# Two narrow self attentions: query and key stacks of 49 fp32r rows, two heads in the two row halves of the array, stacks built in DRAM

## The chip, the cores and the metric

The kernel runs on one core of one Trainium2 chip. The metric is the device time of one execution in microseconds (us); lower is better. The core has five engines with instruction queues of their own: PE (TensorE, matrix multiplication), ACT (ScalarE, activations), DVE (VectorE), POOL (GpSimd) and SP (SyncE, which issues all transfers here). A queue runs strictly in order, and semaphores order the queues among each other.

## The reference, cut to what matters

Four transformer layers follow one another on x of shape (2, 1024, 256). Each is a self attention, a cross attention to 77 context rows, and a two-layer perceptron, each on a modulated layer norm. Layers 0 and 1 are narrow (16 heads of 16 channels), layers 2 and 3 wide (16 heads of 64). This is the self attention of layer 1; that of layer 0 is the same computation:

```python
def _attn(q, k, v):
    q = q.reshape(q.shape[0], q.shape[1], H, HD).transpose(0, 2, 1, 3)   # H = 16, HD = 16
    k = k.reshape(k.shape[0], k.shape[1], H, HD).transpose(0, 2, 1, 3)
    v = v.reshape(v.shape[0], v.shape[1], H, HD).transpose(0, 2, 1, 3)
    scores = jnp.einsum('bhnd,bhmd->bhnm', q, k) * HD ** (-0.5)
    p = jax.nn.softmax(scores, axis=-1)
    o = jnp.einsum('bhnm,bhmd->bhnd', p, v)
    return o.transpose(0, 2, 1, 3).reshape(o.shape[0], o.shape[2], D)
h = _ln(x, ln1_w, ln1_b) * (1 + sc1[:, None, :]) + sh1[:, None, :]
qkv = h @ Wqkv + bqkv
q, k, v = jnp.split(qkv, 3, axis=-1)
x = x + _attn(q, k, v) @ Wos + bos
```

## The kernel before

The whole network is one program. A planner writes one list of steps, `order`: every step has a time in units of a stage's progress, `plan.put(time, ...)`, the list is sorted by these times, and each engine's program walks through the same list and emits what is its part of each step. So the order of each queue is fixed when the kernel is built, and is not changed by how long anything takes.

A narrow self attention is 16 units: two batch rows, four groups g of four heads, two halves of 512 queries. For one unit:

- `max` (32 a unit): a 128 x 512 tile of scores for the running maximum, made on PE (L1091) into one of three PSUM banks, the ring `attn` = banks 4, 5, 7; DVE reduces it to a column (L1761) and frees the bank. `mjoin` joins the two halves of the keys, `mturn` transposes the 16 columns to rows, and SP copies the negated maxima into a row of the query stack.
- `score` (16 a unit): per block of 128 keys (kt) and pair of heads (pr), two 128 x 512 matmuls (the helper `acc`, L1015) into a pair of the banks 0 to 3, followed by the exponential on ACT (L1469, 1,024 columns). The maximum is subtracted by the extra row: row 96 of the query stack holds it, row 96 of the key stack holds ones.
- `av` (8 a unit): the weighing by V (L1194), one 128 x 32 tile in f32 for each of four heads, side by side in the four column quarters of the array.
- `fin`, `sums16`, `norm`, `proj` (L1479, L1213, L1221, L1246 on PE and ACT, L1838 and L1854 on DVE): normalisation and output projection, one unit later, in the same ring of three banks.

The maxima of unit n are spread over the time of unit n - 1 (`max(n - 1.3, 0)` to `n - 0.3`), so on PE they stand between the scores and weighings of the unit before. In the same stretch stand the projections of queries and keys of the second batch row (`p16`), those of the values (`val16`, L1719 on DVE) and the layer norms of the next stage.

Precision: queries and keys are f32 values cut in three bf16 parts; six products of parts are kept. `p16` makes the parts: ACT the first (L1416), DVE the rest and the second (L1711, L1714), POOL the third (L1990). `keep16` writes them to the DRAM tensor `scr_n` (L2115), six transfers of 256 KB for each batch row and chunk of 128 channels. `stack16` reads them back as a stack for four heads: six blocks of 16 rows (`G6Q`, `G6K` say which part stands in which block), 96 rows in all, twelve transfers of 128 KB (L2127). Two stack buffers are used in turn; group g waits for the last score of group g - 2. A row of ones in the key stack is set by DVE (`begin16`, `fill16`: L1681, L1684).

The cross attentions of these layers use the same tiles, with bf16 stacks of 97 rows, and their plan is appended to that of the self attention. The wide layers use fp32r, in which a matmul of 512 columns takes f32 data in one pass; their maxima are L1087. The perceptrons' matmuls are L1015 (up) and L1324 (down), also in fp32r.

## Time and profile before

| | before |
|---|---|
| median of 3 runs | 4522.99 us (4517.64 to 4530.47) |
| profiled execution, its own time | 4537.6 us |
| its span, first to last instruction | 4535.8 us |
| mean granted clock of PE | 0.948 |
| busy: PE, DVE, ACT, POOL | 4070.6, 3010.2, 2076.4, 1349.6 us |

The profile is of one execution of its own. Durations are taken from it, and its own time stands 0.3% above the median of the runs, so a difference worked out in it has to be put on the median. Busy shares are averages over stages that differ much. Matmuls are pipelined: the record of one is longer than its distance to the next, so paces are read from the starts of groups, not from mean durations. PEclk is the granted clock as a share of 2.4 GHz.

### The profile page before, as it was taken

How to read it: one execution, taken by the hardware profiler on the slowest of the kernel's cores; microseconds unless marked ns; L12 is line 12 of the kernel's file. 1: busy time of each engine (PE TensorE's matmuls, PEld its weight loads, DVE VectorE, ACT ScalarE, POOL GpSimd, SP SyncE). 2: the span in 40 equal slices, each digit the busy share in tenths (PEclk: the TensorE clock that was granted, in tenths of full speed). 3: DMA queues.
4: the chain of work that ended last, by engine and by line, in shares of the span. 5: the costliest groups of instructions: out<-in, count | busy, mean ns of one | idle time of the engine just before them, and what ended most of it. 6: DMA issues, size and time to landing. Idle time of an engine off the chain costs nothing.

```text
span 4535.8 us, 55477 instructions
## 1 busy us (share of the span) xinstructions
PE 4070.6 (90%) x20428; PEld 2486.0 (55%) x20428; DVE 3010.2 (66%) x4405; ACT 2076.4 (46%) x3756; POOL 1349.6 (30%) x664
## 2 busy tenths in 40 slices
PE   7999979799998888998999967888999999997889
PEld 5343357634335675555555545666555555546668
DVE  5888755688885666777777844345677777764355
ACT  2656645255564543443444435553444344435541
POOL 1100011100001035655555543321444444441120
PEclk8999989899998999999999978998999999998999
DMA  4223230312323142331333222323232222214220
GB/s 131 39 43 49 44 70 24 56 30 43 47 44 63 32 88 63 66 65 39 65 66 66 63 65 67 70 61 63 69 70 60 67 66 66 60 47 108 68 54 20
DMA packets 151983, 269.28 MB, mean 59 GB/s; under 512 B 34090, under 2 KB 67812, under 8 KB 150688
## 3 DMA queue, kind: packets, MB, share of 16 engines
q1 hardware_dynamic: 151712, 265.72, 27.9%
q8 instruction: 163, 2.67, 0.3%
q14 instruction: 108, 0.88, 0.1%
HBM read 105.01 MB, written 29.64 MB: 30 GB/s over the span
## 4 chain that ended last, share of the span: by engine, by line
PE 38%; DVE 8%; ACT 4%; POOL 4%; issue 4%; SPq 3%; DMA 1%; POOLq 0%; DVEq 0%; ACTq 0%
PE PS L1015 19%; PE PS L1194 7%; PE PS L1087 4%; PE PS L1236 4%; PE PS L1324 2%; DVE t L1757 2%; SPq L2173 2%; ACT t L1490 1%; DVE PS L1829 1%; SPq L2190 1%; POOL t L2035 1%; PE PS L1118 1%; POOL t L2022 1%; POOL t L2008 1%; PE PS L1204 1%
## 5 line engine op out<-in xcount | busy, mean ns | idle before, releaser
L1015 PE MATMUL PS<-t 128*128 128x512 f32 (+4 forms) x7896 | 1988.9, 384 | 160.4 <-ACT t L1469 24.8
L1469 ACT ACTIVATE t<-PS 128x512 f32<-128x512 f32 (+2 forms) x1600 | 1166.9, 750 | 1124.7 <-PE PS L1015 1118.3
L1015 PEld LDWEIGHTS PS<-t 128*128 128x128 f32 (+2 forms) x7896 | 1253.8, 188 | 708.9 <-issue 253.5
L1194 PE MATMUL PS<-t 128*32 128x512 f32 (+2 forms) x4352 | 809.7, 610 | 0.2
L1757 DVE TENSOR_REDUCE t<-PS 128x1 fp32r<-128x1024 f32 x512 | 622.0, 1220 | 281.4 <-PE PS L1087 275.8
L1761 DVE TENSOR_REDUCE t<-PS 128x1 f32<-128x512 f32 x1024 | 651.4, 684 | 73.1 <-PE PS L1091 70.7
L2035 POOL TENSOR_TENSOR t<-t 128x1024 f32<-128x1024 f32 x256 | 617.6, 2412 | 133.6 <-ACT t L1469 106.9
L1091 PE MATMUL PS<-t 96*128 96x512 bf16 x1024 | 370.3, 394 | 34.8 <-DVE t L1761 14.3
L1087 PE MATMUL PS<-t 128*128 128x512 f32 x1024 | 339.9, 415 | 58.8 <-DVE t L1757 36.4
L2031 POOL TENSOR_TENSOR t<-t 128x1024 f32<-128x1024 f32 x64 | 155.0, 2422 | 734.4 <-PE PS L1204 442.1
L1194 PEld LDWEIGHTS PS<-t 128*32 128x32 f32 (+2 forms) x4352 | 170.7, 122 | 329.1 <-issue 324.4
L1972 POOL TENSOR_TENSOR t<-t 128x2048 f32<-128x2048 f32 x24 | 112.0, 4668 | 788.1 <-DMA t<-in_rows 528.6
L1091 PEld LDWEIGHTS PS<-t 96*128 96x128 bf16 x1024 | 97.1, 98 | 358.2 <-DVE t L1761 135.4
L1236 PE MATMUL PS<-t 128*128 128x256 f32 x1024 | 260.3, 399 | 27.5 <-DVE t L1742 10.9
L1850 DVE TENSOR_TENSOR t<-PS,t 128x1024 f32<-128x1024 f32 x128 | 156.3, 1221 | 166.3 <-PE PS L1236 166.3
L1087 PEld LDWEIGHTS PS<-t 128*128 128x128 f32 x1024 | 195.5, 197 | 127.6 <-DVE t L1757 53.3
L1236 PEld LDWEIGHTS PS<-t 128*128 128x128 f32 x1024 | 197.7, 199 | 69.2 <-issue 23.9
L1829 DVE RECIPROCAL PS<-PS 128x256 f32<-128x256 f32 x128 | 224.7, 1755 | 11.8 <-PE PS L1204 11.8
L1324 PE MATMUL PS<-t 128*128 128x256 f32 x1536 | 219.0, 295 | 10.4 <-DVE t L1946 5.8
L1324 PEld LDWEIGHTS PS<-t 128*128 128x128 f32 x1536 | 207.6, 199 | 22.8 <-DVE t L1946 5.5
L1490 ACT ACTIVATE t<-PS,t 128x77 f32<-128x77 f32 x512 | 159.3, 325 | 132.3 <-DVE t L1797 132.1
L1946 DVE TENSOR_TENSOR t<-t 128x512 fp32r<-128x512 f32 x128 | 113.6, 888 | 138.8 <-ACT t L1572 137.5
(131 smaller groups left out, 3804.9 us busy)
## 6 DMA issues: line engine op xcount, KB each, us to landing
t<-t SPq DMA_DIRECT2D x640, 128.0 KB, 2.5
t<-scr_n SPq DMA_DIRECT2D x288, 128.0 KB, 6.4
t<-t SPq DMA_DIRECT2D x128, 256.0 KB, 3.8
scr_n<-t SPq DMA_DIRECT2D x72, 256.0 KB, 2.3
t<-t SPq DMA_DIRECT2D x256, 64.0 KB, 2.0
t<-in_L_Wg SPq DMA_DIRECT2D x16, 768.0 KB, 4.6
t<-in_L_W SPq DMA_DIRECT2D x36, 256.0 KB, 3.2
t<-in_L_Wo SPq DMA_DIRECT2D x64, 128.0 KB, 2.5
```

The costliest lines, as they stand in the source:

```text
L1015: ins = e.matmul(out, l, r, start=i == 0, stop=i == len(terms) - 1, tile_position=tp)
L1087: ins = e.matmul(o[:, 512 * h:512 * h + 512], u.smq[j][qt], u.smk[j][h], start=True, stop=True)
L1091: e.matmul(o, u.smq[j][qt], u.smk[j][half], start=True, stop=True).then_inc(*bank_full[k].inc(nth))
L1194: ins = e.matmul(banks[S.ot][wd * j:wd * j + wd, :], u.v[j][kt], P[0:S.pr, j, :], start=kt == 0, stop=kt == S.nkt - 1, tile_position=(0, w ...
L1236: ins = e.matmul(o[:, 256 * q:256 * q + 256], S.OR[n % 2][:, 128 * q:128 * q + 128], u.wo[:, :], start=True, stop=True)
L1324: ins = e.matmul(banks[4 + q][:, 0:D], l, r, start=m == 0 and t == 0, stop=m == 7 and t == 2)
L1469: e.activation(dst, src, ACT.Exp, scale=S.L.scale).then_inc(*expd.inc((S.i, i)))
L1490: ins = e.activation(S.PQ[n % 3][:, j, t, :], o[:, 256 * t + CT * b:256 * t + CT * b + CT], ACT.Exp, bias=S.NM[n % 3][:, at], accum_out=S. ...
L1757: e.tensor_reduce(S.MT[m % 2][:, S.nqt * j + qt:S.nqt * j + qt + 1], o, AX.X, ALU.max, negate=True).then_inc(*bank_free[k].nth(nth))
L1761: e.tensor_reduce(S.NMX[:, 4 * j + qt, half:half + 1], o, AX.X, ALU.max).then_inc(*bank_free[k].nth(nth))
L1829: e.reciprocal(o[:, hs], o[:, hs]).then_inc(*recip_made.inc((S.i, n, h)))
L2035: e.tensor_tensor(S.AP_[:, :, :], S.AP_[:, :, :], P[1][:, :, :], ALU.add).then_inc(*pool_summed.inc((S.i, n, kt)))
```

## The change

Only the self attentions of layers 0 and 1 change:

- Queries and keys are cut in two fp32r parts in place of three bf16 ones. Three products of parts are kept, so a stack has 48 rows and one for the maximum: 49. Two heads of a group stand in one stack buffer, one in rows 0 to 48, one in rows 64 to 112. A matmul on the second takes tile rows 64 to 127 of the array, one on the first rows 0 to 63. This holds for scores and maxima both.
- The maxima are ordered so that the two heads of a pair alternate. `mjoin` has two buffers for its input, and the maxima are turned to rows in f32.
- `p16` needs ACT for the first part and one DVE instruction for the second; the cast on DVE and the instruction on POOL are gone. The parts go to one of three block buffers `NB`, and a block is written to DRAM after each half of 512 columns, not after both.
- `keep16` writes each part straight to its places in a DRAM tensor `scr_s` that is laid out as the stacks are, (batch row, q or k, head, 64, 1024): six transfers of 256 KB in f32 for each half, twelve for each chunk. `stack16` is two transfers of 1 MB.
- Row 48 of `scr_s` (zeros for queries, ones for keys) is filled at the program's start, rows 49 to 63 by copies of it within DRAM at the beginning of layer 0. The row of ones that DVE set is gone.

```diff
+    STKD = dram("scr_s", (NB, 2, 16, 64, N))
...
-            S.NMX = sbt(c, [128, 16, 2])
+            S.NMX = [sbt(c, [128, 16, 2]) for _ in range(2)]
...
+            S.QK = [q[:, :, :, :].rearrange("p a (x y) n -> p a x (y n)", x=2).bitcast(F32R) for q in S.QKB]
+            S.NB = [flat[:, 2048 * i:2048 * i + 2048].rearrange("p (s n) -> p s n", s=4) for i in range(3)]
...
+                    own = [slice(64 * (j % 2), 64 * (j % 2) + 49) for j in range(4)]
+                    u.smq = [[buf[own[j], 0, j // 2, q0 + 128 * t:q0 + 128 * t + 128] for t in range(4)] for j in range(4)]
+                    u.mrow = [f(buf[64 * (j % 2) + 48:64 * (j % 2) + 49, 0, j // 2, q0:q0 + 512]) for j in range(4)]
...
-                    u.smk = [[buf[0:96, 1, j, 512 * h:512 * h + 512] for h in range(2)] for j in range(4)]
-                    u.st = [[[(buf[0:97, 1, j, 128 * kt:128 * kt + 128], buf[0:97, 0, j, q0:q0 + 512])]
+                    u.smk = [[buf[own[j], 1, j // 2, 512 * h:512 * h + 512] for h in range(2)] for j in range(4)]
+                    u.st = [[[(buf[own[j], 1, j // 2, 128 * kt:128 * kt + 128], buf[own[j], 0, j // 2, q0:q0 + 512])]
...
-            out = [("max", S, m, j, qt, half) for j in range(S.nh) for qt in range(4) for half in range(2)]
+            out = [("max", S, m, 2 * pr + jj, qt, half) for pr in range(2) for qt in range(4) for half in range(2)
+                   for jj in range(2)]
...
+        return [x for half in range(2) for x in (("p16", S, b, ch, half, 0), ("p16", S, b, ch, half, 1), ("keep16", S, b, ch, half))]
...
+                    i = 4 * b + 2 * ch + half
+                    if i >= 3:
+                        w.wait_ge(nat_out[i % 3], (S.i, i - 3))
+                    dst = S.NB[i % 3][:, 2 * qk, :]
...
-                e.memset(S.QK[1][96:97, 1, :, :], 1.0).then_inc(*zeroed.inc(S.i))
...
+                    e.scalar_tensor_tensor(block[:, 2 * qk + 1, :], o, nat16_bias(S, qk, ch), f(block[:, 2 * qk, :]),
+                                           ALU.add, ALU.subtract).then_inc(*bank_free[k].nth(nth))
...
+                            e.dma_start(STKD[b, qk, :, 49:64, :], STKD[b, qk, :, 48:49, :].broadcast_to([16, 15, N])
+                                        ).then_inc(*rest_filled[b].inc(b, 16))
...
+                    for slot, part in enumerate(((0, 0, 1), (0, 1, 0))[qk]):
+                        e.dma_start(STKD[b, qk, 8 * ch:8 * ch + 8, 16 * slot:16 * slot + 16, 512 * half:512 * half + 512],
+                                    f(S.NB[i % 3][:, 2 * qk + part, :])).then_inc(*nat_out[i % 3].inc((S.i, i), 16))
...
+                    src = STKD[g // 4, qk, 4 * (g % 4):4 * (g % 4) + 4, :, :].rearrange("(x y) r n -> (y r) x n", y=2)
+                    e.dma_start(f(S.QK[g % S.nbuf][:, qk, :, :]), src).then_inc(*stacked[g % S.nbuf].inc((S.i, g), 16))
```

The first place is on PE, inside layer 0's self attention, a stretch of one weighing to another. Before (L1091 a maximum, L1015 x2 a pair of scores, L1194 the weighing, L1213 the sums):

```order
L1194 MATMUL PS<-t 32x512 x4
L1091 MATMUL PS<-t 128x512
L1015 MATMUL PS<-t 128x512 x2
L1091 MATMUL PS<-t 128x512
L1213 MATMUL PS<-t 128x4 x4
L1015 MATMUL PS<-t 128x512 x2
L1091 MATMUL PS<-t 128x512 x2
L1194 MATMUL PS<-t 32x512 x4
```

The same place in the change, where L1105 is a maximum, L1029 x2 a pair of scores, L1208 the weighing and L1227 the sums:

```order
L1208 MATMUL PS<-t 32x512 x4
L1105 MATMUL PS<-t 128x512
L1029 MATMUL PS<-t 128x512 x2
L1105 MATMUL PS<-t 128x512
L1227 MATMUL PS<-t 128x4 x4
L1029 MATMUL PS<-t 128x512 x2
L1105 MATMUL PS<-t 128x512 x2
L1208 MATMUL PS<-t 32x512 x4
```

The steps stand where they stood. New is the part of the array: a pair of scores takes the lower, then the upper half, and the maxima alternate between the halves in their own order, whatever stands between them; the sums and the weighing take all rows.

The second place is on SP, at the beginning of layer 0's self attention: the first rows of queue traffic up to the first stack. Before (L2115 writes the parts, L2127 reads the stack):

```order
L2095 DMA t<-in_L_Wo 128x1024 [waits rest3,rest2,rest4,rest1,rest0]
L2097 DMA t<-in_vrows 128x256
L2115 DMA scr_n<-t 128x1024 [waits nat_0] x2
L2115 DMA scr_n<-t 128x1024 [waits nat_1] x2
L2115 DMA scr_n<-t 128x1024 [waits nat_2] x2
L2127 DMA t<-scr_n 16x4x1024 [waits nat_kept0]
L2127 DMA t<-scr_n 16x4x1024 x11
```

In the change (L2138 fills rows 49 to 63, L2162 writes the parts, L2180 reads the stack):

```order
L2130 DMA t<-in_L_Wo 128x1024 [waits rest3,rest2,rest4,rest1,rest0]
L2132 DMA t<-in_vrows 128x256
L2138 DMA scr_s<-scr_s 16x15x1024 [waits row_filled]
L2138 DMA scr_s<-scr_s 16x15x1024
...
L2162 DMA scr_s<-t 8x16x512 [waits bank_free5,nat_0]
L2162 DMA scr_s<-t 8x16x512 x2
L2162 DMA scr_s<-t 8x16x512 [waits bank_free7,nat_0]
...
L2180 DMA t<-scr_s 128x2x1024 [waits rest_filled0,nat_out1,nat_out0]
L2180 DMA t<-scr_s 128x2x1024
```

Four fills (two of them left out here) now stand ahead of the first write, the writes of two half blocks are twelve in place of six, and the stack is two transfers that wait for both half blocks and for the fill.

## Rows read from the trace of the kernel before

**Rows 1.** The page: busy time; then the chain that ended last, by line.
```profile
PE 4070.6 (90%) x20428; PEld 2486.0 (55%) x20428; DVE 3010.2 (66%) x4405; ACT 2076.4 (46%) x3756; POOL 1349.6 (30%) x664
...
PE PS L1015 19%; PE PS L1194 7%; PE PS L1087 4%; PE PS L1236 4%; PE PS L1324 2%; DVE t L1757 2%; SPq L2173 2%; ACT t L1490 1%; DVE PS L1829 1%; SPq L2190 1%; POOL t L2035 1%; PE PS L1118 1%; POOL t L2022 1%; POOL t L2008 1%; PE PS L1204 1%
```

**Rows 2.** Windows: stretch, length, busy us of each engine, clock, DMA share, GB/s.
```profile
110.26:131.50 21.24, 17.56 (x81) 4.46 (x79) 20.97 (x45) 9.80 (x10) 4.51 (x1) 1.00 0.61 74
110.26:581.73 471.47, 454.65 (x2612) 183.68 (x2611) 389.43 (x698) 288.26 (x324) 29.66 (x18) 1.00 0.28 43
905.00:1385.00 480.00, 461.21 (x2606) 184.54 (x2605) 392.30 (x701) 288.77 (x321) 25.16 (x17) 0.98 0.25 39
...
600.00:700.00 100.00, 82.05 (x557) 57.88 (x557) 59.72 (x133) 41.11 (x55) 18.41 (x12) 0.85 0.35 69
```

**Rows 3.** Groups by form, 200 to 500 us: count, busy us, mean ns, idle before.
```profile
L1761 DVE TENSOR_REDUCE t<-PS 128x1 f32<-128x512 f32 x323 | 206.4, 684 | 20.1 <-PE PS L1091 19.4
L1091 PE MATMUL PS<-t 96*128 96x512 bf16 x323 | 113.8, 383 | 4.9 <-DVE t L1711 2.3 <-DVE t L1761 2.2
L1015 PE MATMUL PS<-t 97*128 97x512 bf16 x322 | 94.5, 379 | 0.0
L1015 PEld LDWEIGHTS PS<-t 97*128 97x128 bf16 x323 | 31.4, 101 | 25.7
L1015 PEld LDWEIGHTS PS<-t 128*128 128x128 f32 x92 | 14.4, 189 | 6.1 <-DVE t L1761 3.4 <-ACT t L1519 0.7
```

**Rows 4.** Timeline of PE, layer 0's self attention: start us, us, instruction.
```profile
299.64 0.39 PE L1091 MATMUL PS<-t 96*128 96x512 bf16 x1
299.96 1.06 PE L1194 MATMUL PS<-t 128*32 128x512 f32 x8
300.95 0.98 PE L1015 MATMUL PS<-t 128*128 128x256 f32 x6
...
310.07 0.60 PE L1015 MATMUL PS<-t 97*128 97x512 bf16 x2
310.51 0.38 PE L1091 MATMUL PS<-t 96*128 96x512 bf16 x1
```

**Rows 5.** Timeline of PE: fp32r in layer 3's perceptron and attention; sums of layer 0.
```profile
4425.00 2.97 PE L1015 MATMUL PS<-t 128*128 128x512 f32 x12
4427.81 0.60 PE L1036 MATMUL PS<-t 128*128 128x128 f32 x4
...
3702.56 1.94 PE L1194 MATMUL PS<-t 128*64 128x512 f32 x8
3704.43 0.74 PE L1015 MATMUL PS<-t 128*128 128x512 f32 x2
3705.01 0.63 PE L1087 MATMUL PS<-t 128*128 128x512 f32 x2
...
302.65 0.95 PE L1213 MATMUL PS<-t 128*128 128x4 f32 x8
```

**Rows 6.** Timeline of SP, DVE and PE at the start of layer 0.
```profile
52.41 4.50 SPq L2115 DMA_DIRECT2D scr_n<-t  x6
58.75 5.48 SPq L2127 DMA_DIRECT2D t<-scr_n  x12
...
70.31 3.47 DVE L1684 MEMSET t<- 1x4096 bf16 x1 [0.91 <-issue]
...
75.75 0.65 PE L1091 MATMUL PS<-t 96*128 96x512 bf16 x1
```

**Rows 7.** Windows of 5 us at the program's start, columns as in rows 2.
```profile
15.00:20.00 5.00, 3.50 (x17) 3.51 (x17) 1.97 (x7) 1.46 (x7) 2.57 (x1) 1.00 1.04 425
...
55.00:60.00 5.00, 4.40 (x24) 3.65 (x22) 4.90 (x8) 2.58 (x6) 3.55 (x5) 1.00 0.68 250
...
65.00:70.00 5.00, 2.21 (x11) 1.95 (x10) 4.03 (x16) 0.00 (x0) 1.80 (x2) 0.80 1.09 117
```

**Rows 8.** Timeline of SP and PE at the start of layer 1's self attention.
```profile
847.44 5.48 SPq L2127 DMA_DIRECT2D t<-scr_n  x12
...
862.54 1.89 PE L1091 MATMUL PS<-t 96*128 96x512 bf16 x4 [8.04 <-DMA t<-scr_n]
```

145 lines of the change are left out of this document (88 added, 57 removed).

## The prediction

> **What bounds the kernel now.** I read the page first: TensorE is busy for 90% of the span and leads the chain that ended last, while VectorE is at 66% [rows 1]. Those are averages over twelve stages, and the edit touches two of them, the self attentions of layers 0 and 1. So next I cut the span from the first to the last score of each [rows 2]: 471.5 us and 480.0 us, together 951.5 us for 32 units, 29.7 us a unit. There TensorE is busy 96% (454.7 of 471.5), VectorE 82 to 83% (389.4 and 392.3), ScalarE 61%, and the clock is granted in full. The bound is TensorE, with VectorE 65 us of each stage behind it. The groups of a steady stretch say what fills them [rows 3]: TensorE with maxima (L1091) and scores (L1015, 97 rows), VectorE with the reductions of the maxima (L1761).
>
> How high VectorE can go is shown by the first unit of layer 0, where a statistics pass falls on top of dense maxima: 20.97 of 21.24 us busy, 98.7%, and TensorE only 17.56 [rows 2]. There VectorE is the bound already, and nothing that TensorE saves helps.
>
> **The change part by part.** *Scores and maxima.* In each stage 512 scores and 480 of the 512 maxima lie between first and last score: 992 matmuls. In bf16 they follow one another at 0.22 us (a pair from 310.07 to 310.51) [rows 4]; I take 0.217, so they hold TensorE for 215 us. Removed: 215.
>
> What replaces them is one fp32r matmul each, of 49 rows, on rows 0 to 48 or 64 to 112. Two neighbours in different halves can run together, two in the same half cannot. A matmul of 512 fp32r columns takes 0.234 us (twelve in 2.81, from 4425.00 to 4427.81) [rows 5]. No matmul of before uses half of the rows, so whether the halves overlap is not in this trace. The nearest thing is the column quarters of the weighing by V (L1194): eight instructions, two rounds of four heads, in 0.99 us [rows 4], where eight that ran one after the other at even one cycle a column would need 1.7 us. Hence I take full overlap. The maxima are not always beside their partner, since scores and weighings stand between them: a typical run is maximum, two scores, two maxima, two scores, maximum. Walking through the program's order with the halves as the code gives them, starting each matmul with its predecessor if its half is free, gives 585 turns for the 992, not 496. 585 x 0.234 = 137 us. Added: 137.
>
> Three things work against it. First the weight loads: 189 ns for fp32r, 101 ns for bf16 [rows 3]. They pipeline: eight f32 loads with four-column matmuls pass in 0.95 us, about 0.11 us each [rows 5]. Two a pair are 0.22, as long as the pair itself, so I let them hide, with nothing to spare. Second, behind a change of tile shape a load has nothing to hide under: in the wide layer two fp32r scores after a weighing take 0.58 us (3704.43 to 3705.01) against 0.47 at the steady pace, 0.11 more [rows 5]. The program has 218 such runs a stage: 24 us. Third, half-row runs are now a shape of their own beside full-row matmuls (projection, sums, values): 457 changes of shape in place of 280 in layer 0, 436 in place of 296 in layer 1, so some 160 more a stage. A change into the weighing costs 0.10 us (0.32 from 299.64 to 299.96 against 0.22) [rows 4]. Whether one between half and full rows costs that is not shown: between 0 and 0.10, nearest to the weighing's, so 0.10, 16 us.
>
> The Trainium skill (TensorEngine Tiling (Array Packing), Key Properties) says that changing the tiling mode drains the engine, and counts 64 rows as a mode of their own. By that rule the third item stands, and the forecast with it; without it the forecast would be 32 us lower, 4438.
>
> TensorE's load in a stage: 454.7 - 215 + 137 + 24 + 16 = 417 us. Its lower bound, without second and third, is 377; its upper one, without any overlap, is 454.7 - 215 + 992 x 0.234 + 40 = 512.
>
> *VectorE.* The reductions stay, 32 a unit with records of 684 ns that overlap a little [rows 3]. One cast per projected block goes, two memsets of a single row a stage go (3.47 us each [rows 6]), neither to speak of inside the core. So its load stays at 389 and 392 us, its floor 389.4/0.987 = 395 and 397. Now 417 and 389 stand close, and both meet at the same three banks: a maximum at the head of TensorE's queue waits for a bank that VectorE frees, and all scores stand behind it. Before, with 65 us between them, TensorE idled for 17 us. With 30 between them I take 22 more than the load, 440 a stage; the bounds are 397 and 471. Gain of the cores: 951.5 - 880 = 71 us; I keep 65, since the first unit and those with the next normalisation are VectorE's already.
>
> *Start of layer 0.* Four copies within DRAM, 1 MB each, now go into the same queue ahead of all else, each half block of both kinds is written as six transfers of 256 KB (3 MB for the first chunk, was 1.5), and a stack is 2 MB in two transfers (was 1.5 MB in twelve). Before, writes began at 52.4, stack reads at 58.75, and the first maximum ran at 75.75 [rows 6], reads going at 117 GB/s with the queue full, 16 partitions at a time; big loads reach 425, block writes at least 250 [rows 7]. The new reads fill 128 partitions with 4 KB runs, so I take 250 and 8 us in place of 15. Fills and writes bring 5.5 MB more, 22 us at 250; about 6 of them fit before 52.4, as the writes wait for ScalarE and VectorE until then. 22 - 6 - 7 = 9, plus 3 as copying inside DRAM is not shown at all: 12 us later. Bounds -5 (425 GB/s) and +35 (117). ScalarE also holds the fourth half block until the first has landed; that lies under the wait for the stack.
>
> *Start of layer 1.* Before, stack reads from 847.4, first maximum at 862.54 with 8.04 us idle for the DMA [rows 8]. The reads get shorter by 7, the writes double but start a half block earlier: -3 us.
>
> *Maxima rows.* Behind a 1.5 MB half block in the queue the row of maxima lands late once or twice: +3.
>
> Sum: -65 + 12 - 3 + 3 = -53. The profiled execution took 4537.6 us, the median of three runs 4523.0, 0.3% less: 4484.6 becomes 4470.
>
> **The rivals.** *VectorE's floor is reached.* Speaks for it: 98.7% in the first unit, where TensorE's waits cost VectorE nothing. It needs a TensorE load near 377, that is free changes of shape. Cores at 395 and 397 give -159, in all 4380. Chance 0.12.
>
> *The halves do not overlap* (or loads and streaming share a path, with both loads 0.11 in front of 0.234). This one ends slower: load 512, 57 us a stage more, 4537.6 + 114 + 12 = 4664, in median terms 4650. It decides from the turn: break-even is (215 - 40)/585 = 0.30 us. Speaks for it: two loads are already as long as a turn, and no half-row matmul is on record. Against it: the column quarters. Chance 0.17, with turns between 0.31 and 0.47.
>
> *The block writes run at half the rate.* Their target is cut in 8 heads of 16 rows where it was 128 rows in one; if fewer of the 16 DMA engines take part, 3 MB at 125 in place of 250 GB/s cost 12 us more before the first maximum of layer 0, and some 3 us at each of the later mixed stretches: 4537.6 - 65 + 12 + 12 + 6 = 4503 (the 3 us of layer 1's start and of the rows cancel), in median terms 4488. Nothing in the rows tells the two apart. Chance 0.25. The Trainium skill (DMA: Bandwidth & Descriptors, "Why a DMA increments its semaphore by 16 and not by 1") says that a transfer uses the largest number of engines up to 16 that divides the slowest dimension of both sides; no run here shows it yet.
>
> *The clock, or bank ping-pong, eats the gain.* Where TensorE waits more, as from 600 to 700 us (82% busy), the granted clock is 0.85 on average [rows 2], a mix of 1.2 and 2.4 GHz. A TensorE that waits for VectorE at every bank might lose 5%, 21 us a stage; with the starts that leaves 4510 to 4530. Against it: in the first unit it waits for VectorE all the time and the clock is 1.00. Chance 0.09.
>
> **How the numbers follow.** Forecast with its own range of 4410 to 4508: 0.37, and with half-rate writes, in the same range, 0.25; floor 0.12; gain eaten 0.09; slower 0.17. This kernel's measurement can tell 0.3% (14 us) from no change. Faster 0.74, same 0.09, slower 0.17. The range goes from 4390, just above the floor case, to 4560, which is a turn of about 0.34 us; outside lie the rest of the floor case and most of the slow one, two in ten.
>
> **What would show it.** In the profile after: half-row matmuls of a pair starting together and about 0.24 us a turn; cores of about 440 us with TensorE near 95% and VectorE near 89%; the first maximum of layer 0 near 88 us; waits of the weight loads on VectorE's reductions longer than before. Wrong would be: scores one after the other, VectorE's share unchanged, or a core of over 470 us. The likeliest error is the cost of the closeness of two engines around three banks, 22 us a stage, which I chose and did not read.

## The result

| | before | after |
|---|---|---|
| median | 4526.73 us (4 runs, 4517.64 to 4535.87) | 4585.84 us (4 runs, 4570.11 to 4591.3) |
| ratio, 95% interval | | 1.0127 (1.0111 to 1.0142) |
| profiled execution | 4537.6 us, span 4535.8 | 4590.6 us, span 4588.4 |
| mean granted clock | 0.948 | 0.936 |

Slower by 59 us (the interval of the ratio lies clear of 1), where 53 us less was forecast. The page of the changed kernel:

```profile
PE 4096.7 (89%) x20428; PEld 2541.8 (55%) x20428; DVE 2983.1 (65%) x4370; ACT 2075.1 (45%) x3756; POOL 1313.1 (29%) x632
L1105 PEld LDWEIGHTS PS<-t 49*128 49x128 f32 x1024 | 176.4, 201 | 385.0 <-DVE t L1790 202.8
```

The same loads before, at that time L1091:

```profile
L1091 PEld LDWEIGHTS PS<-t 96*128 96x128 bf16 x1024 | 97.1, 98 | 358.2 <-DVE t L1761 135.4
```

TensorE's share hardly moves. The wait that matters is that of the weight loads of the maxima: they stand 202.8 us behind VectorE's reductions (L1790), where before it was 135.4. The cores, cut from first to last score as in [rows 2], and two stretches inside them (the columns are those of [rows 2]):

```profile
121.01:617.94 496.93, 467.09 (x2619) 208.89 (x2621) 390.00 (x690) 288.24 (x325) 20.46 (x10) 0.95 0.18 55
929.84:1444.21 514.37, 483.05 (x2611) 217.29 (x2613) 392.18 (x692) 288.46 (x322) 15.89 (x9) 0.91 0.16 49
125.00:155.00 30.00, 28.31 (x97) 10.76 (x100) 22.27 (x49) 12.46 (x13) 2.01 (x1) 0.51 0.06 25
300.00:400.00 100.00, 97.44 (x584) 45.74 (x584) 82.64 (x140) 58.29 (x64) 0.00 (x0) 1.00 0.17 61
```

Layer 0's core takes 496.9 us (was 471.5), layer 1's 514.4 (was 479.7, cut at its own first and last score; the window of [rows 2] is rounded to 480). Of the 52.6 us between the two profiled spans, 10.8 lie ahead of the first score of layer 0, 25.5 in its core, -12.0 between the cores, 34.7 in layer 1's core and -6.3 behind it. Two things stand out. VectorE's work is what it was, 390 and 392 us, but its share fell. And the clock: 0.51 from 125 to 155 us, where [rows 2] had 1.00 from 110 to 131 (and the kernel before had 1.00 from 125 to 155 us too), and 0.91 over layer 1's core. From 300 to 400 us it was granted in full. The stretch of [rows 3], from 200 to 500 us, at a clock of 0.98:

```profile
L1105 PE MATMUL PS<-t 49*128 49x512 f32 x302 | 119.6, 467 | 14.8 <-DVE t L1790 6.5 <-DVE t L1728 4.9
```

There 302 maxima were made where before 323 were, and the mean record of one grew from 383 to 467 ns. The counts make the loss look larger than it is at full clock, since the stretch holds 13.6 us at half the clock and an idle time of 4.24 us, shown below.

Cut into units, the two cores show where the time went. A unit runs here from the exponential (ScalarE's instruction behind a pair of scores) that opens it to the one that opens the next, so the sums differ by 1 to 2 us from the cores above. Units are counted from 0:

| us | before | changed | more |
|---|---|---|---|
| layer 0: 12 units with the full clock in both | 352.1 | 358.9 | 6.8 |
| layer 0: unit 2 | 31.4 | 38.2 | 6.9 |
| layer 0: units 0, 10 and 12, clock 0.61, 0.89, 0.94 in the changed kernel, 1.00 before | 90.4 | 101.7 | 11.3 |
| layer 1: 10 units with the full clock in both | 291.1 | 296.3 | 5.2 |
| layer 1: unit 2 | 31.9 | 44.1 | 12.1 |
| layer 1: units 0, 9 to 12, clock 0.59 to 0.94, before 0.90 to 1.00 | 157.7 | 174.6 | 16.9 |

At full clock the changed kernel is slower by 0.5 us a unit; most of the loss lies in a few units. Unit 2 is a case of its own. There VectorE's cast L1689, 0.42 us in the median, took 3.87 us beside an instruction on GpSimd, and ended 0.3 us after it; TensorE stood behind the reduction that followed:

```profile
195.52 4.54 POOL L2001 TENSOR_TENSOR t<-t 128x2048 f32<-128x2048 f32 x1 [68.51 <-DMA t<-in_rows]
196.47 3.87 DVE L1689 CAST t<-t 128x512 fp32r<-128x512 f32 x1
201.72 0.49 PE L1105 MATMUL PS<-t 49*128 49x512 f32 x1 [4.24 <-DVE t L1790]
```

In layer 1 it was L1691, 4.90 us where 0.69 is usual, with 4.99 us of idle TensorE, and both times the clock stood at 0.50 afterwards. In unit 2 of the kernel before no VectorE instruction was held like this, and with the interleaved stacks (below), whose matmuls are the same, none either: the unit took 32.2 and 32.1 us there. So some 18 us of the two cores hang on whether two instructions of other engines meet, and not on the array. No run was made to test it.

The start, first SP's queue and the first maximum, then the DMA (answers to [rows 6, 7]):

```profile
45.77 3.37 SPq L2138 DMA_DIRECT2D scr_s<-scr_s  x4
49.75 16.33 SPq L2162 DMA_DIRECT2D scr_s<-t  x12
75.73 0.90 SPq L2180 DMA_DIRECT2D t<-scr_s  x2
...
83.79 0.79 PE L1105 MATMUL PS<-t 49*128 49x512 f32 x1 [2.78 <-DMA t<-scr_s]
```

```profile
65.00:70.00 5.00, 0.45 (x3) 0.46 (x3) 1.26 (x2) 1.42 (x3) 0.00 (x0) 0.50 0.53 204
70.00:75.00 5.00, 5.00 (x25) 5.00 (x25) 0.15 (x1) 1.45 (x6) 0.00 (x0) 0.50 0.48 186
```

The first maximum runs at 83.8 us (was 75.75). The twelve writes hold the queue until 66, and while the rest of them runs the DMA share is 0.53 and 0.48, as with about half of the 16 engines at work, at 204 and 186 GB/s.

How a run of half-row matmuls goes, in a stretch at full clock. Behind a weighing (L1208) the run begins at 355.08, the next weighing at 357.38; between them nine half-row matmuls, maxima (L1105) and scores (L1029); PEld are the weight loads:

```profile
354.33 3.77 DVE L1790 TENSOR_REDUCE t<-PS 128x1 f32<-128x512 f32 x6
355.08 0.19 PEld L1105 LDWEIGHTS PS<-t 49*128 49x128 f32 x2 [0.84 <-DVE t L1790]
355.08 0.51 PE L1105 MATMUL PS<-t 49*128 49x512 f32 x2
355.19 0.19 PEld L1029 LDWEIGHTS PS<-t 49*128 49x128 f32 x2
355.42 0.40 PE L1029 MATMUL PS<-t 49*128 49x512 f32 x2
355.66 0.18 PEld L1105 LDWEIGHTS PS<-t 49*128 49x128 f32 x1 [0.28 <-DVE t L1790]
355.66 0.49 PE L1105 MATMUL PS<-t 49*128 49x512 f32 x1
355.66 0.29 PEld L1029 LDWEIGHTS PS<-t 49*128 49x128 f32 x2
355.66 0.72 PE L1029 MATMUL PS<-t 49*128 49x512 f32 x2
356.36 0.18 PEld L1105 LDWEIGHTS PS<-t 49*128 49x128 f32 x1 [0.40 <-DVE t L1790]
356.36 1.09 PE L1105 MATMUL PS<-t 49*128 49x512 f32 x2
356.95 0.18 PEld L1105 LDWEIGHTS PS<-t 49*128 49x128 f32 x1 [0.41 <-DVE t L1790]
357.38 0.64 PE L1208 MATMUL PS<-t 128*32 128x512 f32 x4
```

The halves do overlap: the two scores of 355.42 are followed at 355.66, 0.24 us a pair, as forecast. But the run takes 2.30 us and not 5 turns x 0.234 = 1.17 plus a load. At 356.36 one maximum goes, and its partner is held until VectorE (L1790) frees a bank: its load starts at 356.95, 0.19 us pass before it may stream, and only then 0.234 us of matmul. The pair cost 1.02 us. VectorE, in the first row, took six tiles in 3.77 us, 0.63 us each.

### The profile page after: what moved, and what is told of

The parts are those of the page before. It is cut to its first block, busy times and chain, and to the rows that moved or that the text cites. A ratio compares the mean times of both kernels' runs of the same rounds, so it can differ in the third digit from the quotient of the medians.

```text
span 4588.4 us, 55383 instructions
## 1 busy us (share of the span) xinstructions
PE 4096.7 (89%) x20428; PEld 2541.8 (55%) x20428; DVE 2983.1 (65%) x4370; ACT 2075.1 (45%) x3756; POOL 1313.1 (29%) x632
## 4 chain that ended last, share of the span: by engine, by line
PE 61%; DVE 16%; ACT 7%; issue 5%; SPq 4%; POOL 4%; DMA 3%; DVEq 0%; POOLq 0%; ACTq 0%
PE PS L1029 25%; PE PS L1208 13%; PE PS L1105 5%; DVE t L1790 4%; PE PS L1101 4%; PE PS L1250 4%; PE PS L1338 3%; PE PS L1260 2%; DVE t L1784 2%; SPq L2226 2%; PE PS L1235 1%; SPq L2243 1%; PE PS L1227 1%; ACT t L1497 1%; ACT t L1518 1%
## 5 line engine op out<-in xcount | busy, mean ns | idle before, releaser
L1029 PE MATMUL PS<-t 128*128 128x512 f32 (+4 forms) x7896 | 1985.8, 394 | 165.5 <-ACT t L1497 26.4
L1029 PEld LDWEIGHTS PS<-t 128*128 128x128 f32 (+2 forms) x7896 | 1292.1, 200 | 668.1 <-issue 278.2
L1208 PE MATMUL PS<-t 128*32 128x512 f32 (+2 forms) x4352 | 828.7, 628 | 0.4 <-ACT t L1497 0.4
L1790 DVE TENSOR_REDUCE t<-PS 128x1 f32<-128x512 f32 x1024 | 648.8, 683 | 115.9 <-PE PS L1105 110.8
L1105 PE MATMUL PS<-t 49*128 49x512 f32 x1024 | 419.5, 501 | 53.3 <-DVE t L1790 19.2
L1105 PEld LDWEIGHTS PS<-t 49*128 49x128 f32 x1024 | 176.4, 201 | 385.0 <-DVE t L1790 202.8
L1208 PEld LDWEIGHTS PS<-t 128*32 128x32 f32 (+2 forms) x4352 | 171.7, 123 | 316.4 <-issue 311.3
```

The costliest lines, as they stand in the source:

```text
L1029: ins = e.matmul(out, l, r, start=i == 0, stop=i == len(terms) - 1, tile_position=tp)
L1105: e.matmul(o, u.smq[j][qt], u.smk[j][half], start=True, stop=True).then_inc(*bank_full[k].inc(nth))
L1208: ins = e.matmul(banks[S.ot][wd * j:wd * j + wd, :], u.v[j][kt], P[0:S.pr, j, :], start=kt == 0, stop=kt == S.nkt - 1, tile_position=(0, w ...
L1790: e.tensor_reduce(S.NMX[m % 2][:, 4 * j + qt, half:half + 1], o, AX.X, ALU.max).then_inc(*bank_free[k].nth(nth))
```

## The experiments

Times stand beside 4585.8 us for the changed kernel and 4520 to 4527 us for the kernel before, timed again with each; ratios are to the latter. Cores are spans from first to last score, as above. "At full clock" compares, in one profile each, only units to which both kernels had the full clock granted.

### What overlap and the clock are worth

**Both heads of a pair in one half.** Heads 1 and 2 of each group change places; the column quarters of the weighing follow.

```diff
-                    own = [slice(64 * (j % 2), 64 * (j % 2) + 49) for j in range(4)]
+                    own = [slice(64 * (j // 2), 64 * (j // 2) + 49) for j in range(4)]
```

> Heads 0 and 1 of a group share one row half, heads 2 and 3 the other, so both matmuls of a pair use the same rows; the alternation of the maxima is lost too. 815 turns a stage in place of 585, the same 218 and 212 runs and the same changes of shape. Theory 'the halves do overlap and the overlap is worth what I forecast': 230 turns x 0.234 = 54 us more a stage, about 4586 + 108 = 4694. Theory 'the overlap is there, but TensorE's turns are not what bounds the core (banks, weight loads behind a change of shape, the clock)': less than 50 us in all, 4600 to 4635. Theory 'they never overlapped': no change within 0.3%.

**Full rows.**

```diff
-                    own = [slice(64 * (j % 2), 64 * (j % 2) + 49) for j in range(4)]
+                    own = [slice(0, 128) for j in range(4)]
```

> Each score and each maximum reads all 128 rows of its buffer, so both heads' products are summed: the scores are not the reference's, only the time is read. No half-row shape is left (992 turns, each alone; changes of shape back near 280 and 296). Theory 'half-row matmuls let the granted clock fall': from 100 to 200 us the clock comes back from 0.75 to 0.95 or more, and the stretch from 900 to 1000 us too; the first unit of layer 0 takes no longer than before. Theory 'the clock falls for another reason (fp32r, DMA)': it stays below 0.85 there. Theory 'what eats the gain is the entry into a half-row run, 0.43 us in place of 0.22': with the entries gone, 407 more turns (95 us a stage) are paid for by 218 entries x 0.2 (44) and the clock (20), net +30 a stage, about 4640. Theory 'banks and VectorE bound the core': within 20 us of 4586.

Measured: 4809.5 us (ratio 1.062) with one half, 4569.4 (1.011) with full rows. First the one half, cores and the stretch from 125 to 155 us, then the same of full rows:

```profile
120.52:728.77 608.25, 596.65 (x2620) 287.51 (x2622) 393.20 (x690) 290.74 (x325) 20.42 (x10) 0.76 0.15 45
1050.97:1669.75 618.78, 601.58 (x2612) 288.22 (x2614) 398.36 (x692) 290.51 (x321) 15.85 (x9) 0.75 0.13 40
125.00:155.00 30.00, 29.41 (x94) 12.82 (x92) 21.67 (x48) 12.28 (x13) 1.85 (x1) 0.50 0.06 22
```

```profile
119.68:617.00 497.32, 482.90 (x2617) 273.47 (x2616) 394.08 (x691) 288.66 (x324) 20.54 (x10) 0.99 0.18 55
929.91:1424.00 494.09, 481.66 (x2604) 272.17 (x2603) 390.66 (x692) 288.50 (x321) 16.40 (x9) 0.99 0.16 51
125.00:155.00 30.00, 27.75 (x129) 13.09 (x129) 27.30 (x58) 17.27 (x19) 1.96 (x1) 1.00 0.05 20
```

The two kernels run their matmuls in the same order, up to the quarters of the weighing, and a pair of scores overlaps in neither; with one half a maximum and a score still can, 815 turns against 992. Yet the cores are 608 and 619 us against 497 and 494, and the clock is 0.76 and 0.75 against 0.99. From 125 to 155 us TensorE is busy 98% of the time in the first, so it hardly idles, and is still granted half the clock; with full rows it idles more and has all of it. So here work in one row half goes with the low clock, and not the order of the work. The first expectation named 54 us a stage, 3.4 a unit, for the lost overlap; at full clock it is 1.1 us a unit against the changed kernel (six units of layer 0), some 35 us over 32 units by that estimate, and the rest of the 224 us goes with the low clock. For full rows the price of the entries (4640) missed. What came true is the clock, and the theory that banks and VectorE bound the core: within 20 us of 4586, here 16 us *faster* than the changed kernel. In the cores as a whole overlap brings nothing: 0 in layer 0 (497.3 against 496.9), -20 in layer 1, where the clock is 0.99 against 0.91. At full clock it is worth 0.7 us a unit (358.9 against 366.8 us in twelve units of layer 0), and the clock takes that back.

**Only one of the two in halves.** The maxima on 128 rows, the scores in halves, and the reverse:

```diff
-                    u.smq = [[buf[own[j], 0, j // 2, q0 + 128 * t:q0 + 128 * t + 128] for t in range(4)] for j in range(4)]
+                    u.smq = [[buf[:, 0, j // 2, q0 + 128 * t:q0 + 128 * t + 128] for t in range(4)] for j in range(4)]
```

> Scores stay in row halves, always as pairs; the maxima read all 128 rows (two heads' products summed, only the time is read). No single half-row matmul is left, but more changes between half and full rows. Theory 'half-row matmuls hold the clock down': the 992 are half and half now, so the clock of 125 to 155 us rises above 0.50, to 0.75 or 1.0. Theory 'the entry with a single maximum (0.43 us against 0.33) costs most': within the steady stretch of 300 to 400 us more exponentials than the 64 of the changed kernel. Theory 'every change of shape costs': fewer than 61. Total 4550 to 4600.

> The other way round: maxima in row halves, scores on all 128 rows (summed, only the time is read). The maxima rarely have a partner, so overlap is nearly gone and the changes of shape are the most of all. All theories: slower than the changed kernel; by 20 to 50 us if changes cost 0.1 to 0.2 us each (some 250 more changes a stage against none of the 256 score pairs overlapping, 60 us a stage more), about 4640 to 4700. Theory 'clock': half-row matmuls in every run keep it at 0.50 in the first unit.

Measured: 4635.5 us (1.024) and 4752.7 (1.050), both above their ranges, and at full clock 2.2 and 4.4 us a unit more than the changed kernel (12 and 11 units of layer 0). In the first the clock rises as expected (0.89 from 125 to 155 us, 0.97 over both cores), and the cores still take 529 and 530 us; in the second it is 0.65 from 125 to 155 us, not the 0.50 expected. The timeline of TensorE shows why, at full clock:

```profile
351.90 0.50 PE L1029 MATMUL PS<-t 49*128 49x512 f32 x2
352.33 0.51 PE L1105 MATMUL PS<-t 128*128 128x512 f32 x1
352.77 0.50 PE L1029 MATMUL PS<-t 49*128 49x512 f32 x2
```

The pair takes 0.43 us, the full-row maximum behind it 0.44: 0.234 for the columns and 0.19 for a weight load that nothing covers. Every change of shape between half and full rows exposes the load, in both directions. That agrees with the Trainium skill (TensorEngine Tiling (Array Packing), Key Properties), by which a change of the tiling mode drains TensorE; the size of it, a whole fp32r load, is from these rows.

### Who waits for whom

**VectorE's reductions cut** in both kernels, by reading a quarter of each tile of maxima (the result is not the reference's, only the time is read):

```diff
-                e.tensor_reduce(S.NMX[m % 2][:, 4 * j + qt, half:half + 1], o, AX.X, ALU.max)
+                e.tensor_reduce(S.NMX[m % 2][:, 4 * j + qt, half:half + 1], o[:, 0:128], AX.X, ALU.max)
```

> The changed kernel, with one thing left out: VectorE reads 128 of the 512 columns of each tile of maxima, so that each reduction is about 0.35 us shorter (the maximum is taken over a quarter of the keys; only the time is read). Theory 'VectorE and the three banks eat the gain': with some 170 us a stage less on VectorE the waits for banks go, halves pair up, and the cores come down by 50 us or more each, to about 420 to 450. Theory 'TensorE's own entries into runs and the clock eat it': cores fall by less than 20 us each, and the clock of 125 to 150 us stays 0.50.

> The kernel before with the same shortened reductions: the control. TensorE's load there is 455 of 471 us, so by every theory its cores fall by at most 17 to 20 us each, to about 455, total about 4490. The difference to the changed kernel with the same cut is then TensorE's alone: if that one is faster by 20 us or more, the half rows do gain when VectorE does not stand behind them; if it is slower, they lose on TensorE itself.

Measured: 4460.4 us (0.986) and 4463.5 (0.986). The cores of the changed kernel with the cut, then those of before with it:

```profile
115.78:561.62 445.84, 426.79 (x2619) 203.68 (x2621) 212.58 (x690) 285.63 (x325) 20.49 (x10) 0.98 0.20 61
869.21:1318.91 449.70, 433.26 (x2611) 205.43 (x2613) 208.85 (x692) 286.24 (x322) 15.97 (x9) 0.97 0.19 55
```

```profile
107.08:561.00 453.92, 445.92 (x2617) 185.03 (x2619) 213.21 (x698) 287.50 (x325) 29.73 (x18) 1.00 0.29 45
872.51:1327.79 455.28, 444.93 (x2609) 183.87 (x2611) 214.76 (x700) 287.56 (x322) 25.18 (x17) 1.00 0.27 42
```

This pair settles most. With VectorE's part cut, the changed kernel's core is 446 and 450 us, that of before 454 and 455: what TensorE gains is 8 and 6 us a stage, not 38. VectorE's part is the difference to the uncut kernels: 51 and 65 us with half rows, 18 and 24 us with bf16. The control fell by 63 us where 37 were expected, 42 of them in the cores. The low clock is part of the 51 and 65. It can be set apart by the units of layer 0 that had the full clock in all four profiles (1, 3 to 9, 11, 13 to 15):

| us | these 12 units | the other 4 |
|---|---|---|
| before | 352.1 | 121.8 |
| changed | 358.9 | 139.9 |
| before, reductions cut | 343.9 | 112.0 |
| changed, reductions cut | 332.4 | 115.3 |

At full clock TensorE gains 11.5 us in twelve units, and VectorE's part is 26.5 us with half rows, 8.2 with bf16. So the waits for banks take the gain and 7 us more without any help of the clock.

In the changed kernel with the cut the run between two weighings comes close to what it should have been (TensorE only):

```profile
386.44 0.49 PE L1105 MATMUL PS<-t 49*128 49x512 f32 x1
386.45 0.71 PE L1029 MATMUL PS<-t 49*128 49x512 f32 x2
386.79 0.61 PE L1105 MATMUL PS<-t 49*128 49x512 f32 x2
387.02 0.61 PE L1029 MATMUL PS<-t 49*128 49x512 f32 x2
387.32 0.49 PE L1105 MATMUL PS<-t 49*128 49x512 f32 x1
387.74 1.06 PE L1208 MATMUL PS<-t 128*32 128x512 f32 x8
```

Eight matmuls from 386.44 to 387.74, 1.30 us, where four turns and one load would be 1.13: even here the last maximum comes late, its load at 387.32 behind a reduction. Whether a fourth bank in the ring would close that was not tried. Read from the starts in the same way, runs of eight between two weighings take 1.70 us in the changed kernel (median of nine from 300 to 450 us), with the waits, and 1.84 before (ten).

**Full rows, and one half, with the cut:**

> All 128 rows and the shortened reductions together (two heads summed, the maximum over a quarter of the keys; only the time is read). 992 turns, none overlapping, clock free to be full. If overlap saves what its turns say (407 turns x 0.234 = 95 us a stage, less 0.1 to 0.2 us of extra change at some 160 places), the cores are 446 + 95 - 24 = 517 against 446 with half rows, total about 4590. If the full rows with whole reductions (497) were bound by TensorE already, cutting the reductions moves little: 480 to 497 a stage, total 4540 to 4570, and the overlap is worth only 35 to 50 us a stage.

> Both heads of a pair in one row half, with the shortened reductions. Theory 'half-row matmuls hold the clock down by themselves': the clock of the cores stays near 0.75 and 4780 or more, though TensorE no longer waits for VectorE. Theory 'the clock falls because TensorE waits': it comes to 0.95 or more and the total to about 4600, close to full rows with the same cut.

Measured: 4527.5 us (1.0005) and 4708.9 (1.040). The core of layer 0 with full rows, then with one half:

```profile
110.93:595.19 484.26, 474.62 (x2616) 273.65 (x2617) 217.13 (x690) 288.24 (x324) 20.80 (x10) 1.00 0.19 57
```

```profile
117.49:680.92 563.43, 553.13 (x2620) 271.65 (x2622) 217.51 (x690) 289.17 (x325) 20.48 (x10) 0.82 0.16 49
993.07:1566.92 573.85, 563.24 (x2612) 277.66 (x2614) 215.60 (x692) 289.43 (x322) 15.96 (x9) 0.80 0.14 43
```

So with VectorE's part cut overlap is worth 484 - 446 = 38 us in layer 0, 67 us in the two stages together (4527.5 - 4460.4). And the clock of the one half stays low (0.82, 0.80) with VectorE out of the way, so it is not a matter of waits alone; but in the first unit it was 1.00 here, and 0.50 with whole reductions. Both play a part. Of the expectations for full rows the second held for the core and the worth of overlap, the total is 12 us lower; for one half neither held in full; at full clock it costs 1.9 us a unit there (eight units of layer 0), against the 3.4 of its turns.

**One full-row matmul more per block** in the first two units:

```diff
+                    if not S.cross and n < 2 and pr == 0:
+                        e.matmul(pairs[i % 2][0:S.kr, 0:512], u.full[0], u.full[1], start=True, stop=True)
```

> The changed kernel with one more full-row fp32r matmul of 512 columns ahead of each block's scores in the first two units of both narrow self attentions (32 in all; the scores overwrite its result). It costs 32 x (0.23 + 0.2 to 0.4 for two changes) = 14 to 20 us at full clock. Theory 'half rows alone hold the clock at 0.50 there': from 125 to 155 us it is 0.90 or more, a block takes 4.6 to 5.1 us in place of 5.9, and the total is within 10 us of 4586. Theory 'the clock is low there for other reasons': it stays at 0.50 and the total grows by 20 to 30 us.

Measured: 4611.1 us (1.019), and the clock from 125 to 155 us still 0.51, with TensorE busy for 29.19 of the 30 us.

The theory that I held fell; numbers and clock are those of the other one. Since full rows alone did lift the clock, half rows still have a part in it, but a single full-row matmul for each block doesn't undo it.

### Where the maxima stand

Five placements, to have fewer entries into half-row runs. In the plan the maxima of the next unit were put at the scores' times: in pairs; four behind both pairs of scores of a block; one ahead and three behind; two and two; and at four fixed places. The last four use the interleaved stacks of the next section. The form of the edit, here with one ahead (there the maxima also start with the upper half; the steps that join and turn the maxima move a little in all but the first):

```diff
-                        plan.put(max(n - 1.3, 0), n - 0.3, max_steps(S, n))
+                        slots = list(range(8 * n - 10, 8 * n - 2)) if n > 1 else list(range(6))
+                        for i, k in enumerate(slots):
+                            mine = todo[32 * i // len(slots):32 * (i + 1) // len(slots)]
+                            for x, step in enumerate(mine):
+                                plan.put(k / 8 + (-1e-4 if x < 1 else 1 / 24 + 1e-4), 0, [step])
```

> The maxima stand in the plan in pairs, one of each half, at the time of a pair of scores: 496 turns in place of 585, 155 and 149 runs in place of 218 and 212, 80 fewer changes of shape a stage. Theory 'entries into a run and single turns cost the gain': 89 turns x 0.234 = 21 and 63 entries x 0.2 = 13 us less a stage, together about 4586 - 68 = 4518. Theory 'a pair of maxima waits for two of three banks, one after the other, so VectorE sets the pace': 4570 to 4600, with the waits of the weight loads of the maxima on VectorE's reductions longer. Theory 'the clock': it stays near 0.75 from 100 to 200 us, and only some 30 us are gained.

> The stacks of the interleaved kernel (4570), and the maxima of the next unit stand in the plan four for each block of keys, behind both pairs of scores: one run of S S S S M M M M, then the weighing. 498 turns and 155 runs a stage, as with the pairs of maxima. A wait for a bank then stands behind the scores, not ahead of them, but the fourth maximum always waits for VectorE. Theory 'load of TensorE with exposed loads of 0.19 us, plus waits for banks': load about 448 - 63 x 0.19 - 87 x 0.234 = 416 a stage; if waits stay at 50, cores of 465 and about 4505 in all. Theory 'bursts of maxima starve the ring': cores of 490 or more, 4570 or more.

> The same with one maximum ahead of the scores: M S S S S M M M, the maxima alternating from the upper half so that all eight pair up (4 turns). VectorE reduces the three of the last run under the weighing, and the first one here under the scores. Theory 'entries and bank waits': best of the four, cores of 430 to 460 us, total 4450 to 4500, the clock above 0.95. Theory 'half rows hold the clock down whatever the order': the clock of the cores stays below 0.95 and the total above 4530.

> Two maxima ahead: M M S S S S M M. The second one ahead waits for a bank that VectorE holds, with all scores of the block behind it. Theory 'entries and bank waits': between the two others, 4480 to 4540. If it is the slowest, the wait ahead of the scores is what the pairs of maxima lost on (4644).

> The control: the kernel before (bf16 stacks of 97 rows), with the maxima in the same places as M S S S S M M M. Its matmuls do not overlap, and a run costs only 0.10 us to enter: 63 fewer entries are 6 us a stage. Theory 'the order helps by fewer entries into half-row runs': within 15 us of before, 4510 to 4540. Theory 'the order helps by fewer waits for banks, whatever the rows': faster by 20 us or more too.

> Interleaved stacks; the four maxima of a block stand at fixed places: one behind the weighing, one ahead of the first pair of scores, one between the pairs, one behind the second, so most runs are M M S S M S S M with little clumping. Theory 'entries and clumps of maxima both cost': faster than the 4570 of the interleaved stacks with the old spread, 4520 to 4560. Theory 'any locking of maxima to scores costs more in waits for banks than it saves': 4575 to 4640.

| placement | median, us | ratio |
|---|---|---|
| pairs | 4643.8 | 1.027 |
| none ahead, four behind | 4865.3 | 1.075 |
| one ahead, three behind | 4680.8 | 1.034 |
| two ahead, two behind | 4629.6 | 1.023 |
| fixed places | 4629.9 | 1.023 |
| one ahead, three behind, in the kernel before | 4628.4 | 1.023 |

The theory of entries missed in all of them, by 60 us and more, and always to the slow side; the theory of starved banks named the right range for none ahead and for the fixed places. The interleaved stacks with the even spread take 4570.0, so bunching costs 60 to 295 us. With four in a row TensorE is 85% busy from 300 to 400 us and the clock 0.85:

```profile
300.00:400.00 100.00, 84.83 (x419) 39.11 (x419) 60.88 (x104) 42.41 (x47) 0.00 (x0) 0.85 0.17 40
```

The control shows that this is no matter of half rows: the kernel before loses 104 us by the same bunching. At full clock it is 2 us a unit slower (six units of each core), which over 32 units would be some 60 of the 104, an estimate; the rest lies in units with a lower clock. VectorE needs 0.63 us for each tile and the ring has three banks, so what a planner gives up in even spacing comes back as idle time of TensorE, with the scores queued behind, and in these runs as a lower clock too.

**The old order of the maxima**, eight of one head after one another, in one half:

```diff
-            out = [("max", S, m, 2 * pr + jj, qt, half) for pr in range(2) for qt in range(4) for half in range(2)
-                   for jj in range(2)]
+            out = [("max", S, m, j, qt, half) for j in range(S.nh) for qt in range(4) for half in range(2)]
```

> The changed kernel with the maxima in the order of before, all eight of a head after one another, so in one row half: 719 and 734 turns a stage in place of 585. Theory 'alternation is worth its turns': 134 and 149 turns x 0.234 = 31 and 35 us a stage, about 4652. Theory 'most of the pairs of maxima are broken by the wait for a bank anyway': less than 20 us in all, 4590 to 4606. If the granted clock falls with the work packed less densely in the halves, as with both heads in one half, more: above 4660.

Measured: 4669.8 us (1.033), 84 more than the changed kernel, above the 66 of its turns. But from 125 to 155 us the clock is 0.50, and 0.922 over the whole program against 0.936. At full clock the old order costs 0.35 us a unit (272.4 against 269.2 us in nine units of layer 0, and the same in layer 1), where the lost turns alone would be 2. So at full clock the numbers are those of the second theory, by which most pairs of maxima are broken by the wait anyway, and the bulk of the 84 us goes with the lower clock, as the third had it with its "above 4660".

### The start

**Interleaved stacks.** Row 3r + slot in place of 16 x slot + r makes a write one stride over 128 rows; stacks have 48 rows in DRAM, no fills; the maxima use 48 rows, and a stack is read in four transfers.

```diff
-                        e.dma_start(STKD[b, qk, 8 * ch:8 * ch + 8, 16 * slot:16 * slot + 16, 512 * half:512 * half + 512],
+                        dst = STKD[b, qk].rearrange("h (r s) n -> (h r) s n", s=3)
+                        e.dma_start(dst[128 * ch:128 * ch + 128, slot, 512 * half:512 * half + 512],
```

> Stack rows are interleaved (row 3r + slot) so that a block is written as 128 rows at one stride, not as 8 heads of 16 rows; the DRAM stacks have 48 rows, row 48 of the keys comes from the tile of ones, the maxima use 48 rows, and the 4 MB fill of rows 48 to 63 is gone. Stack reads are 48 rows for each half, 4 transfers of 384 KB. Theory 'the writes run on 8 of 16 engines and the fills stand ahead of them': the DMA share of 0.50 from 65 to 75 us goes to 0.9 or more, the first maximum of layer 0 comes at 68 to 74 in place of 83.8 us, time 4570 to 4577. Theory 'the start is not set by the DMA': first maximum within 2 us of 83.8 and time within 5 us of 4586. The cores stay as they are (497 and 514 us) by all theories.

The same without fills and with short reads, but the writes in 8 heads of 16 rows:

> Stacks of 48 rows in DRAM, no fills, reads of 48 rows in 4 transfers, as in the interleaved kernel, but the writes in their changed form, 8 heads of 16 rows. Theory 'the writes run on 8 engines and set the start': the DMA share is near 0.50 from 60 to 70 us and the first maximum of layer 0 comes at 79 to 83 us, against 73.9 with writes over 128 rows; total 4575 to 4585. Theory 'the fills set it': first maximum within 2 us of 73.9 and total near 4570.

Measured: 4570.0 us (1.011) and 4581.1 (1.012). DMA from 50 to 70 us and the first maximum, interleaved, then in blocks:

```profile
50.00:60.00 10.00, 9.25 (x49) 7.83 (x48) 5.25 (x7) 4.85 (x10) 0.00 (x0) 1.00 0.85 315
60.00:70.00 10.00, 6.92 (x44) 6.50 (x43) 4.62 (x22) 1.54 (x6) 0.00 (x0) 0.77 0.85 132
```

```profile
73.86 0.79 PE L1106 MATMUL PS<-t 48*128 48x512 f32 x1 [6.28 <-DMA t<-scr_s]
```

```profile
50.00:60.00 10.00, 8.16 (x39) 6.74 (x37) 3.75 (x5) 3.12 (x5) 0.00 (x0) 1.00 0.45 142
60.00:70.00 10.00, 6.88 (x32) 6.88 (x33) 1.79 (x4) 3.26 (x10) 0.00 (x0) 0.61 0.45 173
```

```profile
83.23 0.79 PE L1106 MATMUL PS<-t 48*128 48x512 f32 x1 [8.65 <-DMA t<-scr_s]
```

With the block writes the DMA share is 0.45 and the first maximum at 83.2 us; with 128 rows in a write it is 0.85, and the first maximum at 73.9. From 50 to 60 us that is 142 GB/s against 315. The fills and the longer reads matter for 0.6 us there (83.8 with them). A share of about half agrees with the Trainium skill (DMA: Bandwidth & Descriptors, "Why a DMA increments its semaphore by 16 and not by 1"): the number of engines is the largest up to 16 that divides the slowest dimension of both sides, here 8. The trace shows the share, not which engines. Layer 1's core took 499 us in the first of these profiles and 504 in the second, with the matmuls of the changed kernel, which took 514. That core varies with the clock, 0.94 in the first and 0.91 in the changed kernel: units at full clock agree within 0.3 us in the sum of ten, while unit 11 took 29.6 us at 1.00 in the first and 38.5 at 0.69 in the changed kernel, and unit 2 32.1 and 44.1, since the instructions of VectorE and GpSimd do not meet there. So of the 16 us between 4570.0 and 4585.8 the start is 10, and the rest can't be put down to the transfers.

## Why the prediction was wrong, step by step

- **Removed 215, added 137 us (585 turns).** The turn was right: a pair takes 0.24 us, the halves overlap. The rival that denies it is out: at 0.24 us a pair neither loads nor columns wait for the other half. With VectorE's part cut, overlap is worth 38 us in layer 0, not the 95 of its 407 turns.
- **Weight loads and changes of shape, 24 + 16 us a stage.** This step was mis-sized. I took 0.11 us for an entry and 0.10 for one of the 160 further changes, from f32 pairs of full rows and from bf16, where part of the load was already under way. A change between shapes costs the whole fp32r load, 0.19 us (a lone maximum takes 0.43 us, was 0.22 to 0.32 in bf16). With the reductions cut, from the first matmul of each run to the next other one, the 218 runs of layer 0's core take 212.5 us; 582 turns (those on record) x 0.234 = 136 of it are columns, so 76 are left, 0.35 a run. The runs of the kernel before take 235.2 us, 987 x 0.217 = 214 of it columns, 21 left. What lies between the runs grew from 218.7 to 233.4. That is 55 + 15 = 70 us on top of the columns in place of 40, and 453.9 - 214 + 136 + 70 = 446, the measured core. 0.19 a run is 41 of the 76; the others hold late banks, as at 387.32, one stall of 4.2 us like that of unit 2, and two stretches of 6.8 us at half the clock; they were not split further. The low clock of these stretches is in the 446 too. So with VectorE's part cut the core fell by 6 to 8 us, not by 38.
- **Coupling of two engines at three banks, +22 us a stage.** The second step that failed, and the larger one. The 22 were 5 more than the 17 of before; by the cut, VectorE's part grew from 18 to 51 us in layer 0 and from 24 to 65 in layer 1, that is by 34 and 40. I argued from how close the two loads are. What the timeline shows is another mechanism: a bank that is late splits a pair, so that both of its matmuls pay for their columns alone, and the second its load too. That is a cost of half rows at full clock as well: 26.5 us in the twelve units where bf16 had 8.2.
- **The clock, put at nothing in the sum.** The third step. Units 0, 10 and 12 of layer 0 and 0 and 9 to 12 of layer 1 took 11.3 and 16.9 us more, with the clock down to 0.59; that this is the clock's is seen by unit 11 of layer 1, 29.6 us at 1.00 and 38.5 at 0.69 with the same matmuls. Unit 2 of both layers, 6.9 and 12.1 us more, is the meeting of VectorE and GpSimd with the low clock behind it, which no term of the sum had. Without what these units lost, the two cores would still have been 12 us slower and not 71 faster: loads and waits alone had eaten the gain.
- **VectorE's floor** was not approached: 390 of 497 us, 78%.
- **The clock rival (0.09)** named 4510 to 4530 and TensorE's waits as its cause. The clock did fall, but to 0.51 where TensorE was 94% busy, and with half rows in one half where it was 98% busy. So its 0.09 was too low and its price too small. I had argued from the first unit of before, where TensorE waited and the clock was 1.00; that was a stretch of 96 and 97 rows and said nothing of half rows.
- **Start of layer 0, +12 us.** Measured +8 for the first maximum and +10.8 for the first score, but for the wrong reason: I booked 9 for fills and writes and 3 for copying in DRAM, and held half-rate writes for a rival on top. The fills with the longer reads cost 0.6 us, the half rate 9.4. That rival was right in its mechanism, and its price of 12 us near.
- **Start of layer 1, -3 us.** Counted from the end of layer 0's core, the first maximum there comes 9.1 us earlier, and the stretch between the cores is 12.0 us shorter.
- **Maxima rows, +3 us.** Not seen: in neither core does TensorE wait for a transfer.
- **The range.** Its upper end, 4560 us, is by the prediction's own sum a turn of 0.32 us, not 0.34. The measured 4585.8 lies above it with a turn of 0.24, so it was the terms beside the turn that were too narrow.
- **What would show it.** Pairs starting together and the late first maximum came true; cores of 440 us and VectorE at 89% (it was 78) did not, and "a core of over 470 us" was the sign of error that I had named.

No version here that computes the reference's result beats the kernel before. The best of them is the one with interleaved stacks, 4570.0 us.

## What to carry to other kernels

Before splitting the array in halves, count the runs and not the matmuls: each run between other shapes pays one whole weight load, so short runs (here four to five matmuls on average) give much of the overlap back. Then look at what feeds and empties the banks: with VectorE at 390 us beside TensorE's 450, pairs were broken by single late banks. A run with that engine's work cut, of both kernels, tells how much of a gain is TensorE's own. Compare unit by unit, and first those at the same granted clock: the whole time put 84 us on an order of the maxima that costs 0.35 us a unit. And spread the tiles that share a small ring evenly; bunching them for TensorE's sake cost 58 to 295 us here.

## What was not expected of the hardware

- Fp32r matmuls in one row half at a time were granted 1.2 GHz from 123 to 246 us without a break, with TensorE 99% busy, where the same order on all rows had 2.4 GHz but for 6.8 us. In the changed kernel, at 0.51 from 125 to 155 us, one more full-row matmul in each block left it at 0.51. With the reductions cut, the same one-half work had full clock from 125 to 155 us and 0.80 to 0.82 over the cores. What exactly decides is open; the number of rows read (49 against 128) and the half differ together in these runs.
- A switch between half-row and full-row fp32r work costs 0.19 us each way, the same whichever comes first (0.43 us for one maximum or one pair).
- DRAM writes over 8 heads of 16 rows ran at a DMA share of 0.45 to 0.53, the same bytes over 128 rows at 0.85.
- A VectorE instruction of 0.42 us took 3.87 us, and one of 0.69 took 4.90, beside one GpSimd instruction of 4.5 us, and both ended 0.3 to 0.6 us after it. Seen, not tested.
